# A delta-rule stage of 64 turns: f32 products written as three products of f16 halves, and a layer norm whose statistics two engines share

## What is computed

```
def _layernorm(x, axis=-1, eps=1e-05):
    return (x - mean(x)) / sqrt(var(x) + eps)
...
query, key_, value = jnp.split(silu(causal_conv(Wqkv @ x)), ...)     # 16 key heads, 32 value heads, width 128
def step(state, inp):
    q_t, k_t, v_t, g_t, b_t = inp          # q, k of unit length; g <= 0; b = sigmoid
    state = state * jnp.exp(g_t)[..., None, None]
    kv_mem = jnp.einsum('bhkv,bhk->bhv', state, k_t)
    delta = (v_t - kv_mem) * b_t[..., None]
    state = state + k_t[..., None] * delta[..., None, :]
    out = jnp.einsum('bhkv,bhk->bhv', state, q_t)
    return (state, out)
...
return (rmsnorm(core) * norm_w * silu(z)) @ Wout.T
```

## Time and profile before

| | us |
|---|---|
| median of 3 runs (lowest, highest) | 3491.84 (3490.82, 3492.23) |
| the profiled execution | 3496.09 |
| its span; mean granted TensorE clock | 3494.4; 0.952 |
| busy in the span: PE / DVE / ACT / POOL | 3089.3 / 2625.7 / 2128.0 / 1517.3 |

### The profile page before, as it was taken

The page is one execution under the profiler, slowest core; times in us unless marked ns, Lnnn a source line. Parts: engine busy times, 40 slices in busy tenths (PEclk is TensorE's granted clock), DMA queues, the critical chain, the costliest instruction groups (busy, mean ns, idle before and its releaser), DMA issues. The chain is left out here.

```text
span 3494.4 us, 77166 instructions
## 1 busy us (share of the span) xinstructions
PE 3089.3 (88%) x29261; PEld 2182.4 (62%) x29280; DVE 2625.7 (75%) x4740; ACT 2128.0 (61%) x5446; POOL 1517.3 (43%) x1853
## 2 busy tenths in 40 slices
PE   6999788447999999999999999999999999993186
PEld 4666565324777777777777777777777777772143
DVE  3444479884878878788787887878878788776887
ACT  4444310135777777777777777777777777764454
...
DMA packets 42858, 118.97 MB, mean 34 GB/s; under 512 B 6032, under 2 KB 10256, under 8 KB 39184
## 3 DMA queue, kind: packets, MB, share of 16 engines
...
...
## 5 line engine op out<-in xcount | busy, mean ns | idle before, releaser
L2030 DVE TENSOR_TENSOR delta_Pb<-delta_bank,delta_lev 128x512 f16<-128x512 f32 x448 | 310.9, 694 | 201.0 <-PE delta_bank L2360 201.0
L1600 POOL TENSOR_SCALAR_AFFINE_SELECT delta_LA<-delta_LA 128x512 f32<-128x512 f32 x128 | 81.6, 637 | 798.6 <-DVE delta_LA L2059 763.6
L2022 DVE SCALAR_TENSOR_TENSOR delta_F<-delta_bank,delta_cw,delta_F 128x510 f32<-128x510 f32 (+1 forms) x512 | 381.5, 745 | 57.8 <-ACT delta_far L1838 40.3
L2334 PE MATMUL delta_bank<-delta_xh,delta_qkvh 128*128 128x512 f16 x1024 | 390.4, 381 | 4.6 <-DVE delta_qkvl L1995 3.1
L2334 PE MATMUL delta_bank<-delta_xl,delta_qkvh 128*128 128x512 f16 x1024 | 390.4, 381 | 0.0
L2334 PE MATMUL delta_bank<-delta_xh,delta_qkvl 128*128 128x512 f16 x1024 | 390.3, 381 | 0.0
L1620 POOL TENSOR_TENSOR delta_F<-delta_F,delta_far 128x506 f32<-128x506 f32 x256 | 278.8, 1089 | 192.7 <-DVE delta_F L2022 192.7
L1832 ACT ACTIVATE delta_F<-delta_bank,delta_cw 128x512 f32<-128x512 f32 x256 | 175.2, 684 | 264.4 <-PE delta_bank L2334 264.2
L2047 DVE CAST delta_XT<-delta_bank 128x512 f16<-128x512 f32 x384 | 263.3, 686 | 85.2 <-PE delta_bank L2379 85.0
L1797 ACT ACTIVATE delta_Xi<-delta_bank 128x512 f16<-128x512 f32 x320 | 190.1, 594 | 155.1 <-PE delta_bank L2375 155.0
L2319 PE MATMUL delta_bank<-delta_zh,delta_xh 128*128 128x256 f16 x1024 | 280.2, 274 | 0.6 <-ACT delta_gz L1860 0.6
...
## 6 DMA issues: line engine op xcount, KB each, us to landing
...
```

The lines of the kernel that those rows point to most:

```text
L2022: ve.scalar_tensor_tensor(dst, src, cw_tap(i, 3 - lag), dst, ALU.mult, ALU.add)\
L2030: ve.tensor_tensor(left(Pb[:, lvl, :, :], lvl), comp(bank[5], lvl), bc(lev[:, lvl, :].rearrange("p (n s) -> p n s", s=1 << lvl), 1, 8), AL ...
L2334: ins = te.matmul(bk[:, :], ww[:, QKV[job], kc, :], xx[:, kc, tok:tok + 512], start=(m == 0), stop=(m == 11))
```

## The change

**Norms.** In `norm_stage` ACT computes mean and variance of tiles 0 to 4 (STATS_BY_ACT = 5): a sum by Identity with an accumulated output, then the squares about the mean. DVE takes the statistics of the other eleven and moves ACT's results into `mv` with two small operations. In the guarded norm ACT scales its five tiles too.

**Delta stage.** `LA` loses its second buffer and becomes six blocks of 128 columns. The blocks A00, A10, L10 and A11 are split into f16 halves: the high half by ACT (`split_high(n)`: `Ah`, `Bh`), the low half by POOL (`split_low(n)`: `Al`, `Bl`); keys and queries likewise (`products_high(i)` on ACT, `products_low(i)` on POOL: `Fh`, `Fl`). The solutions w0 and w1 are kept as f16 halves `W16` and `Wl16`, where `W` held them in f32, so `refined` is a copy of the correction. `products_j0`, `products_j1`, `times_L(1, 0)`, `output_first` and `output_second` become three f16 products for each f32 one: high x high, low x high, high x low. `mask_ge` becomes BF16. `Gb` has one buffer and is loaded one unit later. ACT's last weight chunk and convolution weights move from the end of turn 1 modulo 4 to the start of the next (`next_turns_weights`), and DVE's value_weights(3) moves behind add_out(3). The new waits are on `fl` (products_j0), `alo` (times_L(1, 0), output_second, and DVE's decayed_j0 and decayed_j1, which overwrite the single `LA`) and `ll`.

```diff
+STATS_BY_ACT = 5
...
-            for i in range(NT):
+            for i in range(SA, NT):
                 if guarded:
-                    dve.wait_ge(sca.sem, sca.at(i + 1))
+                    dve.wait_ge(sca.sem, sca.at(i + 1 - SA))
                 ve.bn_stats(st[:, i, :], X[:, i, :]).then_inc(stats.sem, 1)
-            for i in range(NT):
-                dve.wait_ge(stats.sem, stats.at(i + 1))
+            for i in range(SA, NT):
+                dve.wait_ge(stats.sem, stats.at(i + 1 - SA))
                 ve.bn_aggr(mv[:, i, :], st[:, i, :]).then_inc(mom.sem, 1)
...
+            dve.wait_ge(squares.sem, squares.at(SA + 1))
+            ve.tensor_scalar(mv[:, 0:SA, 0], sm[:, 1, :], -1.0, None, ALU.mult).then_inc(moved.sem, 1)
+            ve.tensor_scalar(mv[:, 0:SA, 1], sm[:, 2, :], 1.0 / D, None, ALU.mult).then_inc(moved.sem, 1)
+            dve.wait_ge(mom.sem, mom.at(NT - SA))
+            dve.wait_ge(moved.sem, moved.at(2))
...
+            for i in range(SA):
+                if guarded:
+                    act.wait_ge(sact.sem, sact.at(i + 1))
+                nc.scalar.activation(junk[:, i, :], X[:, i, :], ACT.Identity, accum_out=sm[:, 0, i:i + 1])\
...
-        Gb = sb("Gb", [P, 2, 2, 512])
+        Gb = sb("Gb", [P, 2, 512])
...
-        mask_ge = sb("mask_ge", [P, 256])
+        mask_ge = sb("mask_ge", [P, 256], BF16)
...
+        Fh, Fl = sb("Fh", [P, 2, 2, 256], F16), sb("Fl", [P, 2, 2, 256], F16)
...
-        LA = sb("LA", [P, 2, 4, 2, 384])
+        LA = sb("LA", [P, 4, 768])
+        Ah, Al = sb("Ah", [P, 2, 3, 4, P], F16), sb("Al", [P, 2, 3, 4, P], F16)
+        Bh, Bl = sb("Bh", [P, 4, P], F16), sb("Bl", [P, 4, P], F16)
...
-        W, W16 = sb("W", [P, 2, 4, P]), sb("W16", [P, 4, P], F16)
+        W16, Wl16 = sb("W16", [P, 2, 4, P], F16), sb("Wl16", [P, 2, 4, P], F16)
...
+        L00, L10, A00, A10, A11 = 128, 256, 384, 512, 640
+        split_from = (A00, A10, L10, A11)
+
+        def split_to(n, u, part):
+            return (Bh, Bl)[part][:, :, :] if n == 2 else (Ah, Al)[part][:, u % 2, min(n, 2), :, :]
...
+                def products_low(i):
+                    after("fh", i + 1, 2)
+                    gp.tensor_tensor(Fl[:, :, 1 - i, :], by_half(i), Fh[:, :, 1 - i, :], ALU.subtract)\
+                        .then_inc(g["fl"].sem, 1)
...
                     squares_low(1)
-                    u, par = it.u(2), it.u(2) % 2
-                    pool.wait_ge(g_load[par].sem, g_load[par].at(it.u(2) // 2 + 1, it.kh(2) * 2))
+                    products_low(0)
+                    products_low(1)
...
+                def split_low(n):
+                    after("ahi", n + 1, 1)
+                    if n != 2:
+                        after("o", 2, -1)
+                    else:
+                        after("sv", 4, 0)
+                    by_sequencer()
+                    gp.tensor_tensor(split_to(n, it.u(1), 1), LA[:, :, split_from[n]:split_from[n] + P],
+                                     split_to(n, it.u(1), 0), ALU.subtract).then_inc(g["alo"].sem, 1)
+
                 if it.has(1):
+                    split_low(0)
...
                     conv_far("v1")
+                if it.has(1):
+                    split_low(1)
...
                     low_L(0)
-                    low_L(1)
+                    split_low(2)
...
+                if it.has(1):
+                    low_L(1)
+                    split_low(3)
...
-                    sc.activation(flat(W16[:, :, :]), bank[2][:, :], ACT.Copy).then_inc(g["u0"].sem, 1)
+                    sc.activation(flat(W16[:, k, :, :]), bank[2][:, :], ACT.Copy).then_inc(g["u0"].sem, 1)
+
+                def products_high(i):
+
+                    if not it.has(2):
+                        return
+                    after("silu", i + 1, 2)
+                    after("s", 3, 1)
+                    sc.activation(Fh[:, :, 1 - i, :], by_half(i), ACT.Copy).then_inc(g["fh"].sem, 1)
+
+                def split_high(n):
...
+                    after("la", 8, 1)
+                    if n != 2:
+                        after("o", 2, -1)
+                    else:
+                        after("sv", 4, 0)
+                    sc.activation(split_to(n, it.u(1), 0), LA[:, :, split_from[n]:split_from[n] + P], ACT.Copy)\
+                        .then_inc(g["ahi"].sem, 1)
...
+                def next_turns_weights():
+
+                    if it.u(1) == 3 and it.has(1):
+                        after("qj", 4, 1)
+                        high("qkv", 3, it.kh(1) + 1)
+                        after("taps", 8, 1)
+                        after("far", 4, 1)
+                        conv_weights(it.kh(1) + 1)
...
+                next_turns_weights()
                 level_x(4, 0)
...
                 gate(0)
+                products_high(0)
+                products_high(1)
+                split_high(0)
+                split_high(1)
                 conv_tap("v1")
                 level_x(1, 1)
                 next_qkv(0)
                 next_qkv(1)
+                split_high(2)
+                split_high(3)
                 first_answer(1)
                 gate(1)
                 silu_job("v1")
...
-                next_qkv(3)
-                next_conv()
                 next_z(0)
...
-                    after("o", 2, -1)
+                    after("ll", 1, 0)
+                    after("alo", 3, 0)
...
+                    after("ll", 2, 0)
+                    after("alo", 4, 0)
...
-                    after("u0", k + 1, 0)
-                    ve.tensor_tensor(W[:, k, :, :], W16[:, :, :], heads(bank[2]), ALU.add).then_inc(g["w"].sem, 1)
+                    ve.tensor_copy(flat(Wl16[:, k, :, :]), bank[2][:, :]).then_inc(g["w"].sem, 1)
...
-                value_weights(3)
                 level_p(4, 0)
                 add_out(2, -2)
                 decayed_j0(0)
                 output_variance()
                 level_xt(4, 0)
                 add_out(3, -2)
+                value_weights(3)
                 newton()
...
                         after("ke", 1, 1)
+                        after("fl", 2, 1)
                     else:
                         after("w", 2, -1)
                     bk = bank[(6, 2)[b_]]
-                    kj = F[:, 1, b_ * 256:b_ * 256 + P]
-                    te.matmul(bk[:, 0:256], kj, F[:, 1, b_ * 256:(b_ + 1) * 256], start=True, stop=True)
-                    te.matmul(bk[:, 256:512], kj, F[:, 0, b_ * 256:(b_ + 1) * 256], start=True, stop=True)\
-                        .then_inc(g["s"].sem, 1)
+                    for i, (kj, kq) in enumerate(((Fh, Fh), (Fl, Fh), (Fh, Fl))):
+                        last = te.matmul(bk[:, :], kj[:, b_, 0, 0:P], flat(kq[:, b_, :, :]), start=(i == 0),
+                                         stop=(i == 2))
+                    last.then_inc(g["s"].sem, 1)
...
-                        t0 = b_ * 256 + P
-                        kj = F[:, 1, t0:t0 + P]
-                        te.matmul(bank[6][:, b_ * 256:b_ * 256 + P], kj, kj, start=True, stop=True)
-                        last = te.matmul(bank[6][:, b_ * 256 + P:(b_ + 1) * 256], kj, F[:, 0, t0:t0 + P], start=True,
-                                         stop=True)
+                        out = bank[6][:, b_ * 256:(b_ + 1) * 256].rearrange("p (a i) -> p a i", a=2)
+                        for i, (kj, kq) in enumerate(((Fh, Fh), (Fl, Fh), (Fh, Fl))):
+                            last = te.matmul(out, kj[:, b_, 0, P:2 * P], kq[:, b_, :, P:2 * P], start=(i == 0),
+                                             stop=(i == 2))
                     last.then_inc(g["s"].sem, 1)
...
+                def split_product(out, q, n, k, start, stop):
+                    high, low = (split_to(n, it.u(0), part)[:, q, :] for part in (0, 1))
+                    te.matmul(out, high, W16[:, k, q, :], start=start, stop=False)
+                    te.matmul(out, high, Wl16[:, k, q, :], start=False, stop=False)
+                    return te.matmul(out, low, W16[:, k, q, :], start=False, stop=stop)
...
                     if blk == 1:
+                        after("u0", 1, 0)
                         after("w", 1, 0)
+                        after("alo", 3, 0)
...
                         if blk == 1:
-                            last = te.matmul(out, LA[:, it.u(0) % 2, q, 0, P:2 * P], W[:, 0, q, :], start=True,
-                                             stop=True)
+                            last = split_product(out, q, 2, 0, True, True)
...
-                        last = te.matmul(bank[OUT[0]][:, q * P:(q + 1) * P], LA[:, it.u(0) % 2, q, 1, 0:P],
-                                         W[:, 0, q, :], start=True, stop=True)
+                        last = split_product(bank[OUT[0]][:, q * P:(q + 1) * P], q, 0, 0, True, True)
...
                     after("w", 2, 0)
+                    after("alo", 4, 0)
                     for q in range(4):
                         out = bank[OUT[1]][:, q * P:(q + 1) * P]
```

(5 more changed lines are left out.)

86 lines of the change are left out of this document (49 added, 37 removed).

## The result

The changed kernel takes 3546.92 us (median of 4, 3545.86 to 3548.8) against 3491.33; the ratio is 1.016, 95% interval 1.0147 to 1.0173. The forecast was 3541. Its profiled execution has a span of 3544.1 at a mean granted clock of 0.945.

The account below looks back on a forecast made before the run. TensorE, nearly without gaps, was taken to bound the delta stage. Turns +39, clock +19 and norms -8 gave +50 on the profiled 3496.09: 3546, less 4.25 to the median, forecast 3541; range 3445 to 3625.

Parts of the forecast that it names:

- TensorE's -2.02: Delta stage: f16 products save TensorE 2.02 us a turn, -129 us over 64 turns if nothing else is late.
- DVE at level_b(6), 0.32: TensorE's level_b(6) waits 0.32 us for DVE's chain from level_a(5), so 0.60 is gained there, not 0.92.
- add_out(0), 0.28: The 0.28 us saved in output_first is lost, because w2 matmuls behind it need the bank that DVE's add_out(0) empties.
- POOL's chain into level_a(3): Three subtractions ahead of conv_far("v1") delay ACT's silu and level_x(2); level_a(3) waits 1.6 us, plain turn 36.3, +0.2.
- Turn 2, +0.7: value_weights(3) on DVE ahead of level_p(5) makes the chain to level_b(6) 0.5 us late; turn 36.8.
- Turn 3, +0.35: Two z casts ahead of decays(0) and level_x(3) make level_x(3) end some 0.2 us late; turn 36.5.
- Turn 1, +1.25: Turn 1 modulo 4: later POOL chain, third weight cast and contention up to 0.6 put level_a(3) at 32.6; turn 38.1 us.
- the clock, +1.2 a turn: Half clock after TensorE's standstill in turn 1 costs 1.7 us, counted at 0.7 of that in 16 turns: +19 us.
- Norms, -8: Sharing statistics with ACT saves 1.4 us in each of three norms and 4 in the guarded one; bounds nothing to -10.
- (a): Rival: POOL's chain is not late and DVE's chain sets the plain turn at 34.72; 3395 us, chance 0.15.
- (b): Rival: POOL's EL additions and cju take 0.6 us less and no clock loss: 3484, either alone 3503 or 3522; chance 0.20.
- (c): Rival: the clock also falls in the plain turns, 47 x 1.7 = +80 us, 3621; chance 0.20.

Follow-up runs that it names:

- e1_pool_behind: The changed kernel with POOL's products_low(0), products_low(1) and split_low(0) moved behind conv_far("v1"); 3411.54 us.
- e3_three_more_on_pool: The kernel before with three scratch f16 subtractions added on POOL where the change has its own, and a BF16 mask; 3621.53 us.
- e7_lag_behind: e1_pool_behind with DVE's conv_lag("q") moved from ahead of level_xt(5) and level_p(6) to behind them; 3506.26 us.
- e8_x_first: e1_pool_behind with DVE's add_out(0) moved ahead of refined(1); 3383.41 us.

## Why the prediction held, point by point

The sign, the size and the place were right. The place is not luck: e1_pool_behind and e3_three_more_on_pool show it from both sides. That the sum of +50 meets the 49.7 between the two spans so closely is luck: the turns' own errors went against each other, and the stage's +5.0 ahead of its turns, which the sum did not have, was met by norms that gained more and by small gains elsewhere.

- **TensorE's -2.02.** The new matmuls start 0.056 apart in a long row (24 of `output_second`'s from 1826.30 to 1827.64), not the 0.081 that the prediction cites and sets aside. What is left of it without other waits, 34.72, was measured as 34.66 in e1_pool_behind.
- **DVE at level_b(6), 0.32, and add_out(0), 0.28.** The first as forecast in size (0.58 gained of 0.92), but not as a row with 0.3 idle at `level_b(6)`: 0.21 are lost at the bank of the next projection and 0.11 at `level_b(6)`, both behind DVE's same chain (see e7_lag_behind). The second shows as a row with 0.23 idle behind DVE's X in every plain turn, a product that starts 0.60 behind the one before (1784.56) and so 0.39 late, and e8_x_first got these 0.39 back. They are the 0.28 of the prediction and 0.11 that the kernel before had lost there already, without an idle time in its rows:

```profile
1762.38 0.38 PE L2328 MATMUL delta_bank<-delta_ol,delta_ch 128*128 128x512 f16 x1
1762.71 0.39 PE L2328 MATMUL delta_bank<-delta_oh,delta_ch 128*128 128x512 f16 x1
```

- **POOL's chain into level_a(3).** Right in every link. It came at 30.62 of the turn instead of 30.82, because the additions and cju took 3.81 instead of 3.95 and `conv_far("v1")` started at 28.35 instead of 28.6. In e1_pool_behind, where it does not wait, it comes at 29.16; so the wait costs 1.46 (the row's idle time of 1.21, the tail of 0.16 behind which it is counted, and some 0.07 of waiting for DVE's `delta_t` before it), where I had 1.6. Plain turns: 36.3 forecast, 36.11 to 36.13 measured.
- **Turn 2, +0.7.** Wrong: 36.1. I took DVE's idle ahead of `level_p(5)` to shrink from 0.92 by all of 0.60. But the work in front of it (level_xt(4), add_out(3)) had moved 0.3 earlier as well, so 0.63 was left (the row at 1757.83 above), and `value_weights(3)` fits into it: in the turn from 1828.51 `level_p(5)` starts at 5.66 of the turn, in the plain one at 5.68. The step that failed is the shift: it must be taken of both ends of the idle time, not of one. `value_weights(3)` starts at 1832.99 and takes 0.68, and the level behind it is not later:

```profile
1834.17 0.69 DVE L2114 TENSOR_TENSOR delta_Pb<-delta_bank,delta_lev 128x512 f16<-128x512 f32 x1
```

- **Turn 3, +0.35.** Measured +0.14, at the place forecast: the next turn's `level_a(4)` starts 0.18 late, behind `level_x(3)`.
- **Turn 1, +1.25, and the clock, +1.2 a turn.** Too small. `level_a(3)` was forecast at 32.6 and came at 33.47, because I allowed 0.6 for all that DVE's weight splits do to POOL. The splits did 0.43 in the pair, 0.46 up to the end of the copy and 0.44 in `split_low(0)`, and the pair started at 21.58 of the turn where it starts at 20.61 in a plain one, 1.0 late, not 0.8. Without the clock the turn would be 33.47 + 5.50 = 38.97; it is 40.51 on average, so the clock costs 1.5 and not 1.2; the turns of e3_three_more_on_pool with and without the fall differ by the same 1.5. The granted clock is 0.50 (1.2 GHz) from 1822.9 on, behind a stretch with 0.48 of 3.70 busy, and the pitch of a product of 512 columns is 0.43 there instead of 0.22. Before the change none of the turns 1 to 61 had this. In the plain turns, where nothing was counted, the trace shows the clock at 1.00 throughout; no run tells how much longer their wait could have been.
- **Norms, -8.** Measured -11 in the traces and -12.5 alone. Both lie outside the bounds given (nothing to -10): ACT's passes follow each other after 0.61 (sums) and 0.70 (squares), where I took 0.72, and the guarded norm gave 5.1 instead of 4.
- **Sum.** Turns 0, 2 and 3 were forecast 1.1 too long per four turns, turn 1 1.2 too short: 58 forecast for all of them, 62 measured. The stretch ahead of the stage's turns (+5.0) was not in the sum.

Of the rivals, (a), POOL's chain not late, is what e1_pool_behind makes true, at 3411 for its 3395 (turns 1 modulo 4 are 36.36 there, where -1.42 would make them 35.4). (b) did not come: with the BF16 mask an addition of 512 columns took 1.16 instead of 1.27, and all four with the copy 0.14 less, not 0.6; and the clock did fall. (c) did not come either: in the plain turns the clock stays at 1.00 with a wait of 1.21.
